# Splitting the first expert matrices beside the second attention, and an unrolled router that sends one row a token

## The chip, the cores and the metric

The kernel runs on one core of one Trainium2 chip. The metric is device time in microseconds (us), the median of several runs; lower is better. A core has five engines that each work through their own instructions in order: TensorE (PE, matmuls and transposes), VectorE (DVE), ScalarE (ACT), GpSimd (POOL) and SyncE (SP, which here only starts DMA transfers). They wait for one another through semaphores, and every wait in this kernel is written by hand.

## The reference

Input `x` is 4 x 1024 tokens of 256 floats. Four blocks follow, each added to `x` after a layer norm: cross attention over 64 context tokens (16 heads), a quantised gated feed-forward, a second cross attention (with low-rank additions, and with the last 4 context tokens as a second softmax group), and a mixture of 8 experts, of which each token uses 2:

```python
    def _L1_ffn_ref(x, Wr, br, W1, b1, W2, b2):
        scores = jnp.einsum('bsd,de->bse', x, Wr) + br
        _, topk_idx = jax.lax.top_k(scores, K)          # K = 2, E = 8
        indicator = jax.nn.one_hot(topk_idx, E, dtype=scores.dtype).sum(-2)
        weights = jax.nn.softmax(jnp.where(indicator > 0, scores, neg_inf), axis=-1)
        for i in range(E):
            xi = x * indicator[..., i:i + 1]
            h = jax.nn.relu(jnp.einsum('bsd,dh->bsh', xi, W1[i]) + b1[i])
            yi = jnp.einsum('bsh,hd->bsd', h, W2[i]) + b2[i]
            out = out + yi * weights[..., i:i + 1]
        return out
```

W1 is 8 x 256 x 1024 and W2 is 8 x 1024 x 256.

## The kernel before, in words

The tokens are cut into 32 tiles of 128. The stages run one after the other: first attention, feed-forward, `prepare_attention` for the second attention, `attention` (second), `route`, `experts`. Between two stages all engines meet.

**Second attention.** Each engine runs a step for each k from -4 on. The body for four tiles (NS = 4, j = k mod 4) is the body of a hardware loop, with the first and the last four tiles written out. In step k, PE computes `scores(k+3)`, turns `x` of tile k+4 (`turn_x`), turns the probabilities of tile k (`turn_probs`), and multiplies them out for tile k-1 (`output`). ScalarE normalises tile k+4, copies the scores of k+3 out of PSUM, takes the upper fp16 halves (`high_x`, `high_p`), does the exponentials of k+2 and then `squares`. VectorE does maxima, sums, inverses, the lower halves (`rest_x`, `rest_p`), the residual and the statistics. GpSimd does `normalise(k+1)`, `subtract(k+3)` and `add_bias(k+4)`, in that order (lines 699 and 712). `squares` (L617) reads half of one expert matrix (128 x 1024 floats) each step, loaded by SP into one of two buffers, and adds up its squares in `ssq`, from which later a power-of-two scale for every matrix is made. The matrices are not kept.

**Route.** `partition_all_reduce` on GpSimd (L1351) finds the maxima over the partitions, VectorE makes the scales, GpSimd then writes constants (from L1352). All 32 halves of the expert matrices are loaded again; ScalarE makes the upper fp16 half (`hi`, L1432), VectorE the lower (`lo`, L1511). Between them the 32 tiles are scored in four chunks of eight (`walk`, a hardware loop): VectorE normalises a tile, PE turns and scores it. After a chunk VectorE takes the two best experts of every token (L1551 to L1563), PE counts (L1417, L1418), and VectorE works out where each row goes in the DRAM buffer `xs`, sorted by expert (up to L1592). During the next chunk, for each tile, `rows` normalises again into `pay` (four buffers, two rows a token: one for each expert, with its weight and the token's number), `copy_rows` doubles it, and GpSimd sends 2 x 128 rows by indirect DMA (L1376).

**Experts.** 39 tiles of 256 rows, each by one expert: PE turns the rows, multiplies by W1 (`up`, L1693) and W2 (`down`, L1706), each as three fp16 products; VectorE weighs the result by the row's weight (`mt`, kept by `keep_meta`), and GpSimd adds the rows to the output by indirect DMA (L1810).

## Time and profile before

| | us |
| --- | --- |
| median of 3 runs (1702.17 to 1707.84) | 1704.43 |
| the profiled execution, its own time | 1706.82 |
| its span, first to last instruction | 1705.0 |
| second attention, first PE instruction to last statistics | 861.8 to 1085.1 |
| routing | 1085.4 to about 1255 |
| first and last matmul of the experts' unbroken chain | 1262.2 to 1685.1 |

Mean granted clock of TensorE over the span is 0.848 of full speed. Busy shares of the span are PE 76%, DVE 64%, ACT 46% and POOL 31%. A share is an average over stages with different limits, so each stage has to be read by itself.

### The profile page before, as it was taken

The page shows a single profiled execution, that of the slowest core. Times are in us where ns is not written, and L with a number is a line of the kernel's source. Part 1 is how long each engine was busy: PE and PEld are TensorE (multiplying, and loading weights), DVE is VectorE, ACT ScalarE, POOL GpSimd, SP SyncE. Part 2 cuts the span into 40 slices and gives each one's busy share as a digit, 9 for nine tenths or more (in the row PEclk, how much of TensorE's full clock was granted, in tenths as well). Part 3 has the DMA queues.
Part 4 walks back from the last instruction along what each step waited for, and adds up shares of the span by engine and source line. Part 5 has one row for each costly group of instructions (what it writes and reads, how often), then busy time and mean ns, then how long its engine had stood idle before and what let it go on. Part 6 is the DMA issues. An engine that isn't in the chain of part 4 may idle for free. (4 is left out here: it accounts for less than half of the span.)

```text
span 1705.0 us, 29650 instructions
## 1 busy us (share of the span) xinstructions
PE 1293.8 (76%) x8779; PEld 956.2 (56%) x8780; DVE 1082.7 (64%) x1994; ACT 782.0 (46%) x1138; POOL 527.4 (31%) x426
## 2 busy tenths in 40 slices
PE   5779999349865008679969999533249999999996
PEld 3337777234322007526527777432239999999895
DVE  6947777685587784335647778567635555555553
ACT  0545665055555677100447777343424343444441
POOL 1046777000000000100037777244522333333333
PEclk9979999669999558855779999755569999999998
DMA  5000000100122440140002222384622322222221
GB/s 189 1 4 1 0 0 0 56 1 0 55 111 111 170 144 1 29 111 0 0 28 87 86 86 77 102 280 148 209 95 45 49 39 46 44 48 46 46 44 12
DMA packets 64938, 110.87 MB, mean 65 GB/s; under 512 B 9904, under 2 KB 50960, under 8 KB 64240
## 3 DMA queue, kind: packets, MB, share of 16 engines
q1 hardware_dynamic: 50576, 93.27, 17.3%
q0 software_dynamic: 14304, 16.87, 5.7%
q8 instruction: 32, 0.52, 0.1%
q14 instruction: 26, 0.21, 0.0%
HBM read 74.10 MB, written 37.83 MB: 66 GB/s over the span
## 5 line engine op out<-in xcount | busy, mean ns | idle before, releaser
L1810 POOL DMA_INDIRECT out<-ex_yo,ex_mt x78 | 137.3, 1760 | 314.4 <-DVE ex_yo L1785 181.4
L1735 ACT ACTIVATE ex_hT<-ex_ps_h,e_b1T,e_unscale 128x256 f32<-128x256 f32 x312 | 150.5, 563 | 115.9 <-PE ex_ps_h L1693 115.9
L549 PE MATMUL at_ps_s<-c_M,at_xnT_hi 128*128 (+1 forms) x512 | 163.1, 402 | 20.6 <-issue 13.5
L571 PE MATMUL at_ps_y<-c_VW,at_pT_hi 128*128 (+1 forms) x1024 | 171.1, 273 | 1.3 <-DVE main_x_res L669 1.3
L1693 PE MATMUL ex_ps_h<-ex_xT_hi,e_w_hi 128*128 128x256 f16 x624 | 171.1, 274 | 0.0
L1693 PE MATMUL ex_ps_h<-ex_xT_lo,e_w_hi 128*128 128x256 f16 x624 | 171.0, 274 | 0.0
L1693 PE MATMUL ex_ps_h<-ex_xT_hi,e_w_lo 128*128 128x256 f16 x624 | 171.0, 274 | 0.0
L1706 PE MATMUL ex_ps_y<-e_w_hi,ex_hT_lo 128*128 x624 | 170.1, 273 | 0.0
L1706 PE MATMUL ex_ps_y<-e_w_lo,ex_hT_hi 128*128 x624 | 170.1, 273 | 0.0
L1706 PE MATMUL ex_ps_y<-e_w_hi,ex_hT_hi 128*128 x624 | 170.1, 273 | 0.0
L641 DVE TENSOR_REDUCE at_mx<-at_sc 128x16 f32<-128x960 f32 (+1 forms) x96 | 80.0, 861 | 116.3 <-ACT at_sc L602 116.3
L699 POOL TENSOR_TENSOR at_sc<-at_sc,at_ri 128x960 f32<-128x960 f32 (+1 forms) x96 | 127.3, 1340 | 59.4 <-DVE at_ri L664 59.4
L699 POOL TENSOR_TENSOR at_sc<-at_sc,at_mx 128x960 f32<-128x960 f32 (+1 forms) x96 | 127.3, 1340 | 57.3 <-DVE at_mx L641 57.3
L571 PE MATMUL at_ps_y<-c_VW,at_pT_lo 128*128 (+1 forms) x512 | 139.6, 273 | 0.0
L1209 PE MATMUL gm_bank<-f_WdT,f_xq 128*128 128x256 f16 x576 | 65.7, 279 | 94.5 <-DVE f_xq L1179 94.5
L602 ACT COPY at_sc<-at_ps_s 128x1024 f32<-128x1024 f32 x64 | 64.8, 1013 | 146.5 <-PE at_ps_s L549 146.5
L1209 PEld LDWEIGHTS gm_bank<-f_WdT,f_xq 128*128 128x128 f16 x576 | 57.7, 100 | 102.8 <-DVE f_xq L1179 95.0
L1769 DVE CAST ex_hT_hi<-ex_hT 128x1024 f16<-128x1024 f32 x78 | 58.2, 746 | 80.5 <-ACT ex_hT L1735 80.5
L571 PEld LDWEIGHTS at_ps_y<-c_VW,at_pT_hi 128*128 128x128 f16 x1024 | 100.0, 98 | 12.7 <-issue 1.8
L549 PE MATMUL at_ps_s<-c_M,at_xnT_lo 128*128 (+1 forms) x256 | 102.4, 400 | 0.0
L933 PE MATMUL gm_bank<-f_xq,f_WuT 128*128 (+1 forms) x288 | 71.0, 406 | 35.2 <-ACT gm_stg L971 35.2
L1771 DVE TENSOR_TENSOR ex_hT_lo<-ex_hT,ex_hT_hi 128x1024 f16<-128x1024 f32 x78 | 95.6, 1225 | 2.7
(273 smaller groups left out, 2914.0 us busy)
## 6 DMA issues: line engine op xcount, KB each, us to landing
at_half<-in_L_ffn_W SPq DMA_DIRECT2D x32, 512.0 KB, 3.6
rt_stage<-in_L_ffn_W SPq DMA_DIRECT2D x32, 512.0 KB
up_scratch<-gm_stg SPq DMA_DIRECT2D x16, 768.0 KB, 3.2
gm_stg<-up_scratch SPq DMA_DIRECT2D x16, 768.0 KB, 4.3
ex_row<-xs SPq DMA_DIRECT2D x39, 258.0 KB, 2.7
main_x_res<-in_x SPq DMA_DIRECT2D x8, 512.0 KB, 12.2
out<-main_x_res SPq DMA_DIRECT2D x4, 1024.0 KB
xs<-rt_pad SPq DMA_DIRECT2D x18, 129.0 KB
```

Source lines behind the costliest of these rows:

```text
L549: last = nc.tensor.matmul(ps_s[j][:, c * CH:(c + 1) * CH], a[:, d, :], b[:, d, bass.ds(off + c * CH, CH)], start=(n == 0), stop=(n == 3 * ...
L571: last = nc.tensor.matmul(ps_y[:, 0:D], a[j][:, n, :], b[:, bass.ds(off + n * D, D)], start=(n == 0 and i == 0), stop=(n == NP - 1 and i = ...
L602: nc.scalar.copy(sc[j][:, :, :], ps_s[j % 2][:, :].rearrange("p (h k) -> p h k", h=H)).then_inc(ev_r, 1)
L641: last = nc.vector.tensor_reduce(mx[:, j, :, g], sc[j][:, :, lo:hi], AX.X, ALU.max)
L699: last = nc.gpsimd.tensor_tensor(part, part, what[:, j, :, g].unsqueeze(2).to_broadcast([P, H, hi - lo]), op)
L933: last = nc.tensor.matmul(ps[:, o, :], a[:, d, o * P:(o + 1) * P], b[:, d, bass.ds(c0, CH)], start=(n == 0), stop=(n == 3 * DT - 1))
L1209: last = nc.tensor.matmul(ps[:, i, 0:D], a[k % 2][:, at], b[:, o, :], start=(o == 0 and n == 0), stop=(o == FT - 1 and n == 2))
L1693: last = nc.tensor.matmul(ps_h[:, n, :], a[:, bass.ds(e * WN + d * HID + n * P, P)], b[:, d, :], start=(m == 0), stop=(m == 3 * DT - 1))
L1706: last = nc.tensor.matmul(ps_y[j][:, q, :], a[:, n, q * P:(q + 1) * P], b[:, bass.ds(e * WN + n * D, D)], start=(n == 0 and m == 0), stop= ...
L1735: last = nc.scalar.activation(hT[:, n, :], ps_h[:, n, :], ACT.Relu, bias=b1T[:, bass.ds(e * HT + n, 1)], scale=unscale[:, 0, bass.ds(e, 1)])
L1771: nc.vector.tensor_tensor(hT_lo[j][:, part, :], hT[:, part, :], hT_hi[j][:, part, :], ALU.subtract).then_inc(hlo_r, 1)
L1810: nc.gpsimd.indirect_dma_start(out=acc[:, :], out_offset=bass.IndirectOffsetOnAxis(ap=mt[j][:, q, 1:2].bitcast(U32), axis=0), in_=yo[j][:, ...
```

## The change

Five edits that belong together.

1. The memory of W1 in fp16 (`w1`) is reserved before the second attention. While `prepare_attention` runs, its weight buffers lie in it (`arena`).
2. In the second attention, expert e's W1 halves and W2 halves are loaded in the four steps of group e (tiles 4e to 4e+3). The W1 halves stay in their buffers. When their squares are known, VectorE adds the two sums (`scale_of`, j = 2), GpSimd takes the maximum over the partitions (j = 3, ahead of `normalise`), VectorE makes the scale from it (`scale_from`, j = 3, ahead of `rest_p`), ScalarE writes the upper halves (`high_w`, j = 3) and VectorE the lower ones (`low_w`, j = 0 of the next group).
3. `route` is written out instead of looped, splits only W2 (16 halves), and ScalarE normalises straight into the buffer that is sent (`pay`, two buffers of eight tiles). Two sends a tile remain, now both from the same row.
4. A row carries 4 extra values: the first expert's number, (first weight - second weight), second weight, token.
5. In `experts`, `keep_meta` works out the weight from the row and the tile's expert.

```diff
@@ attention, SyncE
+                load_half(1, 0, 0)
+                load_half(0, 0, 0)
+                load_half(0, 0, 1)
+                sp.wait_ge(ssq_r, 1)
+                load_half(1, 0, 1)
+                with nc.sync.Fori(1, E, 1) as e:
+                    sp.wait_ge(ssq_r, 4 * e)
+                    load_half(1, e, 0)
+                    for h in range(2):
+                        sp.wait_ge(wlo_r, 2 * e + h - 1)
+                        load_half(0, e, h)
+                    sp.wait_ge(ssq_r, 4 * e + 1)
+                    load_half(1, e, 1)
@@ attention, ScalarE
+            def high_w(e, h):
+                act.wait_ge(scale_r, e + 1)
+                nc.scalar.activation(w1[0][...], half[h][:, :], ACT.Copy, scale=scale1[:, 0:1]).then_inc(whi_r, 1)
+            def weights(e, j):
+                if j == 0:
+                    squares(e, 1, 0)
+                elif j == 1:
+                    squares(e, 0, 0)
+                    squares(e, 0, 1)
+                elif j == 2:
+                    squares(e, 1, 1)
+                else:
+                    high_w(e, 0)
+                    high_w(e, 1)
@@ attention, VectorE
+            def scale_from(e):
+                dve.wait_ge(all_s, e + 1)
...
             def step(k, j):
                 if there(k - 2, NT):
                     residual(k - 2)
+                if experts_w and j == 0 and there(k - NS, NT):
+                    low_w(k // NS, 0)
+                    low_w(k // NS, 1)
+                if experts_w and j == 2 and there(k, NT):
+                    scale_of(k // NS)
...
+                if experts_w and j == 3 and there(k, NT):
+                    scale_from(k // NS)
                 if there(k, NT):
                     rest_p(k, j % 2)
@@ attention, GpSimd
             def step(k, j):
+                if experts_w and j == 3 and there(k, NT):
+                    pool.wait_ge(sum_s, k // NS + 1)
+                    pool.sem_inc(asked, 1)
+                    nc.gpsimd.partition_all_reduce(bmr[:, :], bm[:, :], P, RMAX).then_inc(all_s, 1)
                 if there(k + 1, NT):
                     normalise(k + 1, (j + 1) % NS)
@@ route, GpSimd
+            for t in range(NT):
+                c, i = divmod(t, TK)
+                pool.wait_ge(meta_r, c + 1)
                 for k in range(2):
+                    g.indirect_dma_start(out=xs[:, :], out_offset=bass.IndirectOffsetOnAxis(ap=pos[c % 2][:, i, k:k + 1], axis=0),
+                                         in_=pay[c % 2][:, i, :], in_offset=None, bounds_check=last_row,
+                                         oob_is_err=True).then_inc(sent[c % 2], 16)
@@ route, ScalarE
+            def norm(t):
+                c, i = divmod(t, TK)
+                if i == 0:
+                    need(act, sent[c % 2], 32 * TK * (c // 2))
+                nc.scalar.activation(pay[c % 2][:, i, 0:D], x_res[:, t, :], ACT.Identity, bias=nmr[:, t:t + 1],
+                                     scale=rstd[:, t:t + 1]).then_inc(xn_r, 1)
...
+            norm(0)
+            for t in range(NT):
+                if t + 1 < NT:
+                    norm(t + 1)
+                copy(t)
+                if t == 2:
+                    act.wait_ge(wsc_r, 1)
+                if t % TK in HIGHS:                     # (2, 4, 6, 7)
+                    high(4 * (t // TK) + HIGHS.index(t % TK))
+                if t % TK == 1 and t > TK:
+                    ratio(t // TK - 1)
+            ratio(NK - 1)
@@ route, VectorE
+            for m in range(NK):
+                if m:
+                    place(m - 1)
+                for q in range(4 * m, 4 * m + 4):
+                    low(q)
+                choose(m)
+            place(NK - 1)
@@ experts, VectorE
             def keep_meta(i, j):
+                e = look_up(nc.vector, 1, i, E - 1)
                 need(dve, added, 16 * Q * (i - 1))
                 dve.wait_ge(meta_r, i + 1)
-                nc.vector.tensor_copy(mt[j][:, :, :], meta[j][:, :, :]).then_inc(mt_r, 1)
+                need(dve, mt_r, i)
+                nc.vector.scalar_tensor_tensor(out=first[:, :, :], in0=meta[j][:, :, 0:1], scalar=eid[:, bass.ds(e, 1)],
+                                               in1=meta[j][:, :, 1:2], op0=ALU.is_equal, op1=ALU.mult).then_inc(first_r, 1)
+                nc.vector.tensor_copy(mt[j][:, :, 1:2], meta[j][:, :, 3:4])
+                dve.wait_ge(first_r, i + 1)
+                nc.vector.tensor_tensor(mt[j][:, :, 0:1], first[:, :, :], meta[j][:, :, 2:3], ALU.add).then_inc(mt_r, 1)
```

`choose` is the work of L1551 to L1563 on a whole chunk, `place` that of L1567 to L1592.

## Rows read from the trace of the kernel before

**Rows 1.** The page, busy time of one engine over the span, share, instructions.

```profile
PE 1293.8 (76%) x8779; PEld 956.2 (56%) x8780; DVE 1082.7 (64%) x1994; ACT 782.0 (46%) x1138; POOL 527.4 (31%) x426
```

**Rows 2.** The chain that ended last, in order of time: start, us, what.

```profile
1262.19 1.12 PE ex_ps_t L1679 x4
...
1679.82 5.25 PE ex_ps_y L1706 x48
```

**Rows 3.** Stretches: us, busy PE, PEld, DVE, ACT, POOL (xcount), PEclk, DMA share, GB/s.

```profile
933.00:985.00 52.00, 52.00 (x384) 38.69 (x383) 40.10 (x81) 40.00 (x67) 40.28 (x41) 1.00 0.28 89
1084.00:1256.00 172.00, 48.35 (x210) 43.38 (x209) 107.53 (x467) 60.37 (x103) 74.48 (x75) 0.51 0.58 185
```

**Rows 4.** Timeline of one tile of the second attention: start, us, engine, line.

```profile
951.86 0.38 PE L537 MATMUL at_ps_xT<-main_ident,at_xn 128*128 128x128 f32 x2
952.08 1.04 PE L560 MATMUL at_ps_p<-main_ident,at_sc 128*128 128x128 f32 x8
...
955.57 0.59 PE L549 MATMUL at_ps_s<-c_M,at_xnT_hi 128*128 x2
...
958.16 0.38 PE L537 MATMUL at_ps_xT<-main_ident,at_xn 128*128 128x128 f32 x2
```

**Rows 5.** The same tile on POOL; in brackets the idle time before and its releaser.

```profile
954.54 2.08 POOL L699 TENSOR_TENSOR at_sc<-at_sc,at_mx 128x960 f32<-128x960 f32 x2 [0.53 <-DVE at_mx L641]
956.58 0.73 POOL L712 TENSOR_TENSOR main_x_res<-main_x_res,at_bias 128x256 f32 x1
```

**Rows 6.** Lines 712 and 1351, the queue's own instructions: duration ns, first and last start.

```profile
L712 POOLq MODIFY_POOL_CONFIG  x4: 11/11/11, 85.5 to 861.2; - x4
L1351 POOLq MODIFY_POOL_CONFIG  x2: 11/11/11, 1089.0 to 1089.0; - x2
```

**Rows 7.** Timeline of POOL: what it ran next after those, and after L1351.

```profile
92.77 0.71 POOL L712 TENSOR_TENSOR main_x_res<-main_x_res,at_bias 128x256 f32<-128x256 f32 x1 [45.63 <-issue]
...
870.28 0.71 POOL L712 TENSOR_TENSOR main_x_res<-main_x_res,at_bias 128x256 f32<-128x256 f32 x1 [40.45 <-issue]
...
1095.18 0.43 POOL L1351 PARTITION_ALL_REDUCE rt_bmr<-rt_bm  x1 [18.30 <-issue]
1102.70 0.14 POOL L1352 IOTA rt_eid<- 128x8 f32 x1 [7.08 <-issue]
```

**Rows 8.** Stretches of 2 us after TensorE had stood still (columns as rows 3).

```profile
871.00:873.00 2.00, 1.69 (x5) 0.69 (x6) 0.16 (x1) 0.00 (x0) 2.00 (x3) 0.61 0.00 0
873.00:875.00 2.00, 2.00 (x7) 0.72 (x6) 0.00 (x0) 0.00 (x0) 0.70 (x2) 0.54 0.00 0
...
1266.00:1268.00 2.00, 2.00 (x15) 1.54 (x13) 0.00 (x0) 0.00 (x0) 0.00 (x0) 0.66 0.51 139
```

**Rows 9.** Timeline, the end of the second attention.

```profile
1074.81 2.08 POOL L699 TENSOR_TENSOR at_sc<-at_sc,at_ri 128x960 f32<-128x960 f32 x2 [1.42 <-DVE at_ri L664]
...
1084.66 0.43 DVE L674 BATCH_NORM_STATS2 main_stats<-main_x_res 128x6 f32<-128x256 f32 x1
```

**Rows 10.** Timeline of the routing on DVE and POOL, first chunk, first reuse, last send.

```profile
1092.55 0.22 DVE L1472 COPY e_b1T<-rt_ps_r 128x64 f32<-128x64 f32 x1 [4.08 <-PE rt_ps_r L1389]
...
1114.36 0.64 DVE L1551 MAX8 rt_top<-rt_scores 128x8 f32<-128x8 f32 x8
...
1122.87 0.18 DVE L1592 CAST rt_pos<-rt_posf 128x16 uint32<-128x16 f32 x1
...
1125.65 1.33 POOL L1376 DMA_INDIRECT xs<-rt_pay,rt_row  x1 [21.36 <-issue]
...
1133.83 0.41 DVE L1460 TENSOR_SCALAR rt_pay<-main_x_res,main_mv,main_rstd 128x256 f32 x1 [0.83 <-DMA xs<-rt_pay,rt_row]
...
1246.90 0.97 POOL L1376 DMA_INDIRECT xs<-rt_pay,rt_row  x1 [0.30 <-issue]
```

**Rows 11.** Groups by line: count, busy us, mean ns, idle before and releasers.

```profile
L1376 POOL DMA_INDIRECT xs<-rt_pay,rt_row x64 | 72.5, 1133 | 71.0 <-issue 38.1 <-ACT rt_pay L1437 22.5 <-DVE rt_row L1521 10.5
L1511 DVE SCALAR_TENSOR_TENSOR e_w_lo<-rt_stage,rt_wsc,e_w_hi 128x1024 f32 (+1 forms) x32 | 41.1, 1284 | 7.1 <-ACT e_w_hi L1432 6.1 <-issue 0.7
```

More of the change, by code:

```diff
@@ L497, in attention @@
         if experts_w:
-            half = [s.sb(f"half{j}", [P, WN // 2]) for j in range(2)]
-            half_in = [s.sem(f"half_in{j}") for j in range(2)]
-            ssq_r, arrived = s.sem("ssq_r"), s.sem("arrived")
+            half = [s.sb(f"half{j}", [P, WN // 2]) for j in range(3)]
+            half_in = [s.sem(f"half_in{j}") for j in range(3)]
+            bm, bmr, scale1 = s.sb("bm", [P, 1]), s.sb("bmr", [P, 1]), s.sb("scale1", [P, 1])
+            asked = s.sem("asked")
+            ssq_r, arrived, sum_s, all_s, chain, scale_r, whi_r, wlo_r = (
+                s.sem(n) for n in ("ssq_r", "arrived", "sum_s", "all_s", "chain", "scale_r", "whi_r", "wlo_r"))
         block = s.block()
@@ L1235, in route @@
         b1r = s.sb("b1r", [E * HT, P])
-        xn = s.sb("xn", [P, 2, D])
+        pay = [s.sb(f"pay{j}", [P, TK, ROW]) for j in range(2)]
         xt = [s.sb(f"xt{j}", [P, DT, P]) for j in range(2)]
@@ L1258, in route @@
         hp, hs = s.sb("hp", [P, E]), s.sb("hs", [P, E])
-        pay = [s.sb(f"pay{j}", [P, 2, ROW]) for j in range(NB)]
-        row_i = [s.sb(f"row{j}", [P, 2], U32) for j in range(NB)]
         pad = s.sb("pad", [P, ROW])
@@ L1326, in _ @@
-            with nc.sync.Fori(1, 2, 1) as e:
-                for j in range(2):
-                    load_matrix(e, j)
+                need(sp, wlo_r, q - NS + 1)
+                sp.dma_start(stage[q % NS][:, :].rearrange("p (t n) -> p t n", n=src.shape[2]),
+                             src[q // 2, (q % 2) * rows:(q % 2 + 1) * rows, :].rearrange("(t p) n -> p t n", p=P)
+                             ).then_inc(half_in[q % NS], 16)
+            for q in range(NS):
+                load_half(q)
@@ L1332, in _ @@
                              x_res[:, g * NT // B:(g + 1) * NT // B, :]).then_inc(acc_in, 16)
-            with nc.sync.Fori(2, E, 1) as e:
-                for j in range(2):
-                    load_matrix(e, j)
+            for q in range(NS, 2 * E):
+                load_half(q)
             sp.wait_ge(cst, CONSTS)
@@ L1402, in score @@
                 for d in range(DT):
-                    last = nc.tensor.matmul(ps_r[j][:, 0:E], xt[j][:, d, :], wr[:, d, :], start=(d == 0), stop=(d == DT - 1))
+                    last = nc.tensor.matmul(ps_r[c % 2][:, i * E:(i + 1) * E], xt[t % 2][:, d, :], wr[:, d, :],
+                                            start=(d == 0), stop=(d == DT - 1))
                 last.then_inc(sc_mm, 1)
-            def tile_step(i, r, t, half):
-                if t is not None:
-                    turn(t, i % 2)
-                    if i >= 1:
-                        score(t - 1, 1 - i % 2)
@@ L1454, in _ @@
+            for t in range(NT):
+                if t + 1 < NT:
[8 more added lines that the diff above has]
+            ratio(NK - 1)
         @block.vector
@@ L1523, in tile_step, with low @@
-            def tile_step(i, r, t, half):
-                if r is not None:
-                    rows(r, i)
-                if t is not None:
-                    norm(t, i % 2)
-                    if i >= 2:
-                        score(t - 2, i - 2)
-                if half:
-                    lo(*half)
-            LINKS = 15
-            def chunk_step(c):
-                for i in range(TK - 2, TK):
-                    score(TK * c + i, i)
-                dve.wait_ge(sc_r, TK * (c + 1))
-                k = [0]
-                def then(ins):
-                    k[0] += 1
-                    ins.then_inc(link, 1)
-                    dve.wait_ge(link, LINKS * c + k[0])
-                    dve.sem_inc(linked, 1)
-                dve.sem_inc(linked, 1)
+            def low(q):
+                dve.wait_ge(whi_r, q + 1)
+                v.scalar_tensor_tensor(out=half_of(1, q), in0=stage[q % NS][:, :], scalar=wsc[:, 1, q // 2:q // 2 + 1],
+                                       in1=half_of(0, q), op0=ALU.mult, op1=ALU.subtract).then_inc(wlo_r, 1)
@@ L1551, in chunk_step @@
                     last = v.max(out=top[:, i, :], in_=scores[:, i, :])
-                then(last)
+                link_on(last)
                 v.tensor_tensor(wt[:, 0, :], top[:, :, 1], top[:, :, 0], ALU.subtract).then_inc(d_r, 1)
@@ L1622, in experts @@
         row = [s.sb(f"row{j}", [P, Q, ROW]) for j in range(2)]
-        meta = [s.sb(f"meta{j}", [P, Q, 2]) for j in range(2)]
+        meta = [s.sb(f"meta{j}", [P, Q, 4]) for j in range(2)]
+        first = s.sb("first", [P, Q, 1])
         mt = [s.sb(f"mt{j}", [P, Q, 2]) for j in range(2)]
```

309 lines of the change are left out of this document (144 added, 165 removed).

## The prediction

> **What bounds the kernel now.** I read the page first, then the chain that ended last, then stretches of single stages, then timelines inside them. The page gives PE 76% of the span [rows 1], which is an average. The chain says more: from 1262.2 to 1685.1 it is nothing but PE, matmul after matmul [rows 2]. Nothing that the change adds to VectorE's 39 steps there can cost time as long as it stays within VectorE's slack. So the change has to be judged in the two stages ahead of the experts, which are bound differently [rows 3]. In the second attention PE is busy 52.0 of 52 us at full clock, with VectorE at 40.1, ScalarE at 40.0 and GpSimd at 40.3. In the routing PE has 48 of 172 us at a clock of 0.51 (its lower level, 1.2 GHz), and no engine is full: VectorE has 107.5, ScalarE 60.4 and GpSimd 74.5. Work moved from the routing into the attention goes from a stage where engines wait for each other into one that has 12 us in 52 left on each engine but PE.
>
> A tile of that attention lasts 6.30 us (951.86 to 958.16): `turn_x` 0.22, `turn_probs` and `output` 3.49, `scores` 2.59 [rows 4]. GpSimd's share is 2 x 2.08 + 0.73 = 4.89 us, and the last of it ends 957.31 - 951.86 = 5.45 us after the scores that it needed, through ScalarE's copy and VectorE's maxima [rows 4, 5].
>
> **The change part by part.**
>
> *The reduction on GpSimd inside the attention.* This decides. The line that reduces over partitions is preceded in GpSimd's queue by MODIFY_POOL_CONFIG, and so is the first elementwise instruction of each attention, which follows such a reduction [rows 6]. The instruction itself takes 11 ns, but what comes next is late: 85.5 to 92.77 is 7.3 us, 861.2 to 870.28 is 9.1, 1089.0 to 1095.18 is 6.2, and after the reduction at 1095.61 the first constant starts at 1102.70, 7.1 later [rows 6, 7]. I read this as GpSimd changing its resident code, 6.2 us towards the reduction and 7.1 to 9.1 back (mean 7.8). Before, nobody waits long for it, since it happens between stages. After the change the reduction stands between elementwise work in every group of four tiles, so both switches come in each: 6.2 + 0.43 + 7.8 = 14.4 us in which GpSimd does nothing else (13.7 to 15.7). It is followed in the queue by `normalise`, `subtract` and `add_bias`; for `normalise` waits `turn_probs`, and with it PE.
>
> The Trainium skill ("GPSIMD Engine Reference", 2.1 Instruction dispatch) says that the first call into freshly loaded code costs about 6 us (5.95) with no instruction to be seen. The trace agrees for the way there and shows 1.1 to 3.1 us more for the way back. By the page a group would lose 2.1 us less, and the sum below would be 15 lower.
>
> How much of 14.4 us reaches PE? Let the stall begin after step K-1. PE has then still two tiles' work, 12.6 us, counted from the end of the scores that GpSimd's last step used, and those ended 5.45 us before. So it runs 7.2 us into the stall and stops at `turn_probs(K+1)`. Count from the stall's end. `normalise` takes 2.1. PE then needs `turn_probs` and `output` (3.49), `scores` (2.59), 0.22, again 3.49 and 2.59 until the last scores of the group: 12.4. It starts after 9 us of standing still, so at the lower clock. Two restarts of before show for how long: from 871.31 to about 874.8 (0.54 over the stretch that ends at 875) and from 1262.19 to about 1267.4, thus 3.5 to 5.2 us, in which half the speed is lost: 1.7 to 2.6, I take 2.2 [rows 2, 8]. Then 5.45 until GpSimd's last instruction, and the next stall begins: 2.1 + 12.4 + 2.2 + 5.45 = 22.15. GpSimd's own work, 4 x 4.89 = 19.6, is less, so PE's restart sets it. With the stall a group takes 36.5 us, against 4 x 6.30 = 25.2: +11.35. Groups 0 to 6 have elementwise work after the reduction: 7 x 11.35 = +79.5.
>
> In group 7 only the way there counts, but `scale_from` stands ahead of the last `rest_p` in VectorE's queue and `low_w` ahead of the last residual. Before, the last `normalise` ended at 1076.89 and the last statistics at 1085.09 [rows 9]. After: 1076.9 + 6.2 + 0.43, some 0.9 for four small operations, 1.3 `rest_p`, PE's 2.6 at the lower clock 5.2, 0.9 for residual and statistics: 1091.8, so +6 (by the full clock +4).
>
> *The splits in the attention.* Per group ScalarE and VectorE each get two passes over 128x1024, 2 x 1.28 by VectorE's row, and VectorE about 0.9 more for the scale [rows 11], on top of 19.4 each in 25.2 [rows 3]. Both fit, and they lie in the stall: `scale_from` waits for the reduction, 6.6 us into it, `high_w` and `low_w` end before it is over. Cost 0; if the stall were not there, they would still fit, at most 2 us a group if `low_w` delays an inverse that GpSimd waits for. The number of squares is as before. The loads are as many bytes as before, each asked for about a tile ahead of its use: 0.
>
> *Routing.* Before, the 64 sends take 72.5 us plus 0.3 each, 91.7, and GpSimd idles 31.4 between chunks (22.5 + 10.5 less the 0.3s) [rows 11]. They begin at 1125.65 [rows 10]. After, chunk 0 no longer passes through VectorE. b1 is turned by 1092.6 as before, then PE and ScalarE need about 1.7 us a tile (an estimate: ScalarE has two passes over 128x256, 0.41 each on VectorE, and half of one of 1.28, and hands over to PE twice), so the last scores stand near 1107 instead of 1114. The fourth `low` ends by 1108.8. `choose` and `place` took from just before 1114.36 to 1123.05, about 9: 1117.9. Nothing like `rows` follows, so sends begin near 1118, 7.7 earlier. But `pay` holds two chunks, and `norm(16)` stands on ScalarE ahead of `copy(15)`: the second chunk can't be scored until all sends of the first have landed, and the third's transfers hold up chunk 3's end in the same way. Landing: the first buffer was free at 1133.83, 8.2 us after its two sends began, of which 2.6 to 3.6 were the sends; I take 4.8. From there: normalise and copy 1.0, `high(7)` and `low(7)` 1.28 each, `choose` and `place` 9: 12.6. So GpSimd stands 17.4 us twice, 34.8 against 31.4, and not a third time (chunk 3 is placed while chunk 2 is sent). Net -7.7 + 3.4 = -4.3. Bounds: if every send takes 0.97 + 0.3 as the last does [rows 10], -10 more, so -15; if a tile takes 2.1 us and a gap 20, +4. The first reduction finds its code resident, which only brings the scales 2 us forward, ahead of need.
>
> *Experts.* Three small VectorE operations of about 0.17 for one, +0.35 us on a tile whose PE work takes 10.9 [rows 2]: 0. If VectorE were the bound it would be 39 x 0.35 = 14. The rows are 0.8% longer: 0.
>
> Sum: +79.5 + 6 - 4.3 = +81.2. On the profiled execution's own 1706.82 that is 1788.0; the median of the runs is 2.4 lower, which gives 1785.6; I forecast 1785.
>
> **The rivals.**
>
> *A: the switches cost nothing in the loop.* Both pieces of code stay resident, or the reduction is reached without the pair of switches. For it: the trace has no reduction between elementwise instructions, so none was seen in a loop. Against: all four such neighbours in the trace are 6.2 us or more apart [rows 6, 7]. Then PE stays the attention's bound, +2 at its end, and the routing's -4 to -15 shows: 1704.4 + 2 - 4 = 1702 down to 1704.4 - 15 = 1689, in the middle 1696. This is the other side. It decides from the point where a stall falls below about 7 us, since PE has 7.2 us of work in hand.
>
> *B: only one of the two directions costs.* Stall 7.8: PE waits 2.7, keeps its clock, and a group takes 2.1 + 12.4 + 5.45 + 7.8 = 27.7: +2.5, 7 times 17.5. 1704.4 + 17.5 + 4 - 4 = 1722. For it: the shorter numbers could be a queue draining; against, the way there and the way back are both seen.
>
> *C: the clock does not come back inside a group.* Standing still 9 us in 36, PE might get 0.5 all through: 12.4 more on its path instead of 2.2, so +10.2 x 7 = 71: 1785 + 71 = 1856. Against: both restarts came back to 1.0 within 5.2 us [rows 8]. The Trainium skill ("TensorE: Matmul & The Clock Gate", HAM oscillation) has kernels that start every pass cold because each is followed by a wait; by that rule this case would lie between my forecast and C.
>
> *D: GpSimd's own work is the bound.* PE restarts at full clock and VectorE or ScalarE are never late: period 19.6 + 13.7 = 33.3, +8.1 x 7 = 57, +4 - 4: 1761.
>
> **How the numbers follow.** Forecast 0.76, A 0.05, B 0.05, C 0.06, D 0.08. The forecast's own range: stall 13.7 to 15.7 is -5 to +9, clock loss 1.7 to 2.6 is -4 to +3, routing -10 to +9, so 1766 to 1806. With D, part of C and steps that I have left out: 1752 to 1826 for 8 in 10. A change within 0.3% (5 us) could not be told from none in a kernel whose three runs spread by 5.7. Faster is A, 0.05; same, 0.01; slower 0.94.
>
> **What would show it.** Right: in the attention's timeline GpSimd has two gaps of 6 to 9 us around each of eight reductions (one at the eighth), PE stands about 9 us in a group, the clock dips once a group, and the stage is longer by 80 to 90 us. In the routing the sends come in three blocks (16, 16, 32) with two gaps near 17 us. The experts' chain is unbroken and as long as before. Wrong: no gap beside the reductions (A); one only (B); PE at 0.5 through the stage (C); a send block before 1110 in the old stage's time, or three gaps, or `ex_ps_h` waiting for VectorE.

## The result, and the profile after

The changed kernel takes 1774.14 us (median of 3 runs, 1772.86 to 1775.33) against 1704.43: a ratio of 1.041, 95% interval [1.038, 1.044], so 69.7 us slower. The forecast was 1785 with 1752 to 1826 as its range. In some executions, of the kernel before too, the second attention begins 12 or 13 us later, which has nothing to do with the change, so what follows is read mainly by the lengths of stages.

| stage (profiled execution of each) | before | after | predicted |
| --- | --- | --- | --- |
| second attention, first PE instruction to last statistics | 223.3 | 313.4 (+90.2) | +85.5 |
| last statistics to first matmul of the experts' chain | 177.1 | 154.2 (-22.9) | -4.3 |
| experts' unbroken chain | 422.9 | 423.1 | 0 |

The total is 11 us below the forecast. It came that close partly by luck: the attention was underestimated by 4.7 us and the routing's gain by 18.6, and the two errors have opposite signs.

Below is the page of the changed kernel, busy time of one engine over the span (beside [rows 1]): the sums have hardly moved, and nothing in them tells of 70 us.

```profile
PE 1317.9 (74%) x8779; PEld 969.1 (55%) x8780; DVE 1072.1 (60%) x1961; ACT 787.2 (44%) x1138; POOL 519.8 (29%) x434
```

The stretch of 147 us in the middle of the second attention shows it (columns as in [rows 3], where 52 us had PE at 52.0): PE is busy for 76% of it, and its mean granted clock is 0.86.

```profile
943.00:1090.00 147.00, 111.16 (x725) 79.34 (x724) 91.12 (x185) 85.88 (x136) 77.01 (x82) 0.86 0.18 56
```

The cause stands in GpSimd's queue. First the queue's own instructions (duration, first and last start), to be held against [rows 6]. MODIFY_POOL_CONFIG comes in pairs: 16 times ahead of the eight reductions, and 14 times ahead of the elementwise product that follows seven of them (behind the eighth no elementwise work is left in the stage).

```profile
L793 POOLq MODIFY_POOL_CONFIG  x16: 8/14/22, 905.8 to 1160.3; - x16
L793 POOL PARTITION_ALL_REDUCE at_bmr<-at_bm x8: 377/377/378, 911.6 to 1165.9; - x8
L774 POOLq MODIFY_POOL_CONFIG  x14: 82/83/83, 911.9 to 1135.3; - x14
```

Then GpSimd's timeline around one of them (beside [rows 5, 7]). `add_bias` ends at 979.39. Six microseconds later the reduction runs for 0.38 us, and 6.71 us after that the next product. Between 979.4 and 992.5 GpSimd does 0.38 us of work.

```profile
978.66 0.73 POOL L787 TENSOR_TENSOR main_x_res<-main_x_res,at_bias 128x256 f32 x1
985.40 0.38 POOL L793 PARTITION_ALL_REDUCE at_bmr<-at_bm  x1 [6.01 <-issue]
992.49 2.07 POOL L774 TENSOR_TENSOR at_sc<-at_sc,at_ri 128x960 f32<-128x960 f32 x2 [6.71 <-DVE at_ri L707]
```

The bracket names VectorE, and that needs a look, because VectorE's own work stands behind the reduction too: the scale, `rest_p`, the residual, `low_w`, the sums, and only then the inverse `at_ri` that the product needs.

```profile
992.12 0.33 DVE L707 RECIPROCAL at_ri<-at_sm 128x32 f32<-128x32 f32 x1
```

Here the inverse ends at 992.45 and GpSimd starts 0.04 us later, so in this one group VectorE may set the end of the wait. In all seven groups the inverse comes 6.5 to 6.7 us after the reduction, and in the other six GpSimd starts 0.24 to 0.83 us after it. The first experiment settles what GpSimd alone needs.

And TensorE through the same stall, against [rows 4]. It stands still twice: 3.72 us until ScalarE's norm, 4.86 until GpSimd's product. The eight transposes that took 1.04 us take 1.94, since the clock is at its lower level (the stretches below), and the next tile's transposes start 9.08 us later in place of 6.30.

```profile
989.52 0.44 PE L555 MATMUL at_ps_xT<-main_ident,at_xn 128*128 128x128 f32 x2 [3.72 <-ACT at_xn L609]
994.81 1.94 PE L578 MATMUL at_ps_p<-main_ident,at_sc 128*128 128x128 f32 x8 [4.86 <-POOL at_sc L774]
...
1003.89 1.04 PE L578 MATMUL at_ps_p<-main_ident,at_sc 128*128 128x128 f32 x8
```

Stretches of 2 us (beside [rows 8]) show when the clock falls and when it is back: 1.00 until 990, 0.50 from 992 to 1000, 1.00 from 1002.

```profile
988.00:990.00 2.00, 0.44 (x2) 0.20 (x2) 2.00 (x3) 2.00 (x3) 0.00 (x0) 1.00 0.00 0
990.00:992.00 2.00, 0.00 (x0) 0.00 (x0) 2.00 (x4) 0.64 (x2) 0.00 (x0) 0.55 0.66 176
...
998.00:1000.00 2.00, 2.00 (x12) 1.41 (x10) 0.11 (x1) 1.95 (x4) 2.00 (x3) 0.50 0.00 0
1000.00:1002.00 2.00, 2.00 (x14) 1.34 (x13) 0.60 (x2) 0.00 (x0) 2.00 (x3) 0.89 0.63 167
```

The end of the attention (against [rows 9]): VectorE waits 5.89 us for the last reduction, works off the scale, and stands 2.74 again for PE's last output. From the end of the last normalisation to the end of the last statistics it is 15.0 us; before it was 8.2.

```profile
1166.30 0.15 DVE L727 TENSOR_SCALAR at_scale<-at_bmr 128x1 f32<-128x1 f32 x1 [5.89 <-POOL at_bmr L793]
...
1174.08 0.48 DVE L712 SCALAR_TENSOR_TENSOR main_x_res<-at_ps_y,c_unscale,main_x_res 128x256 f32<-128x256 f32 x1 [2.74 <-PE at_ps_y L589]
1174.60 0.43 DVE L717 BATCH_NORM_STATS2 main_stats<-main_x_res 128x6 f32<-128x256 f32 x1
```

The routing on GpSimd, against [rows 10]: the first send of each of the three blocks (16, 16 and 32 sends), then the instruction on ScalarE that opens the third chunk, 1.5 us after the first block's last send ended at 1225.03.

```profile
1203.69 2.07 POOL L1408 DMA_INDIRECT xs<-rt_pay,rt_pos  x1 [7.62 <-DVE rt_pos L1594]
...
1237.54 1.76 POOL L1408 DMA_INDIRECT xs<-rt_pay,rt_pos  x1 [12.51 <-DVE rt_pos L1594]
...
1271.18 1.75 POOL L1408 DMA_INDIRECT xs<-rt_pay,rt_pos  x1 [12.72 <-DVE rt_pos L1594]
```

```profile
1226.52 0.60 ACT L1460 ACTIVATE rt_pay<-main_x_res,main_nmr,main_rstd 128x256 f32<-128x256 f32 x1 [18.98 <-DMA xs<-rt_pay,rt_pos]
```

The group of the sends, answering to the first of [rows 11]: 65.2 us in place of 72.5, and 51.5 us of idle time before them in place of 71.0 (7.6 of the 51.5 lie ahead of the first send).

```profile
L1408 POOL DMA_INDIRECT xs<-rt_pay,rt_pos x64 | 65.2, 1019 | 51.5 <-DVE rt_pos L1594 32.9 <-issue 18.6
```

The experts' chain, as in [rows 2], is unbroken and as long as before.

```profile
1329.25 1.11 PE ex_ps_t L1685 x4
...
1747.13 5.25 PE ex_ps_y L1712 x48
```

### The profile page after: what moved, and what is told of

Its sections match the earlier page's. It is cut to its first block and busy times, and to the rows that moved or that the text cites. A ratio compares the mean times of both kernels' runs of the same rounds, so it can differ in the third digit from the quotient of the medians.

```text
span 1772.4 us, 29247 instructions
## 1 busy us (share of the span) xinstructions
PE 1317.9 (74%) x8779; PEld 969.1 (55%) x8780; DVE 1072.1 (60%) x1961; ACT 787.2 (44%) x1138; POOL 519.8 (29%) x434
## 5 line engine op out<-in xcount | busy, mean ns | idle before, releaser
L589 PE MATMUL at_ps_y<-c_VW,at_pT_hi 128*128 (+1 forms) x1024 | 186.0, 287 | 5.6 <-DVE main_x_res L712 5.6
L567 PE MATMUL at_ps_s<-c_M,at_xnT_hi 128*128 (+1 forms) x512 | 161.6, 399 | 20.7 <-issue 13.5
L589 PE MATMUL at_ps_y<-c_VW,at_pT_lo 128*128 (+1 forms) x512 | 146.3, 286 | 0.0
L589 PEld LDWEIGHTS at_ps_y<-c_VW,at_pT_hi 128*128 128x128 f16 x1024 | 105.5, 103 | 21.9 <-issue 6.1
L578 PE MATMUL at_ps_p<-main_ident,at_sc 128*128 128x128 f32 x512 | 72.9, 290 | 43.2 <-POOL at_sc L774 43.2
L1732 ACT ACTIVATE ex_xT_hi<-ex_ps_t 128x512 f16<-128x512 f32 x39 | 23.3, 597 | 182.4 <-PE ex_ps_t L1685 182.4
L1773 DVE SCALAR_TENSOR_TENSOR ex_xT_lo<-ex_ps_t,ex_xT_hi 128x512 f16<-128x512 f32 x39 | 26.9, 690 | 124.0 <-ACT ex_xT_hi L1732 124.0
```

The source lines that it names most:

```text
L567: last = nc.tensor.matmul(ps_s[j][:, c * CH:(c + 1) * CH], a[:, d, :], b[:, d, bass.ds(off + c * CH, CH)], start=(n == 0), stop=(n == 3 * ...
L578: last = nc.tensor.transpose(ps_p[:, n, :], sc[j][:, 2 * n:2 * n + 2, :], ident[:, :])
L589: last = nc.tensor.matmul(ps_y[:, 0:D], a[j][:, n, :], b[:, bass.ds(off + n * D, D)], start=(n == 0 and i == 0), stop=(n == NP - 1 and i = ...
L1773: nc.vector.scalar_tensor_tensor(out=xT_lo[j][:, :, :], in0=ps_t[:, :, :], scalar=XN_SCALE, in1=xT_hi[j][:, :, :], op0=ALU.mult, op1=ALU.s ...
```

## The experiments

Ratios are to the kernel before, run beside each on the same chip. The lengths compared are the attention from PE's first instruction in it to the last statistics (223.3 before, 313.4 after), a group of four tiles from reduction to reduction (four tiles of 6.30, 25.2, before; 37.2 after, (1134.94 - 911.55)/6), and the routing.

Two theories on the attention's 90 us. The first is the prediction's: GpSimd changes its code twice a group. The rival: the splits of W1 crowd ScalarE and VectorE, and the tiles wait for them.

**The reductions alone, in the kernel before.**

```
+                if experts_w and j == 3 and there(k, NT):
+                    nc.gpsimd.partition_all_reduce(red[:, :], one[:, :], P, RMAX).then_inc(red_r, 1)
                 if there(k + 1, NT):
                     normalise(k + 1, (j + 1) % NS)
```

> The kernel before, plus one partition_all_reduce of a one-column tile on GpSimd in the second attention, ahead of the normalisation of every fourth tile (eight in all); nothing waits for its result, and nothing else is changed. Theory 1 (changes of code alone): groups of four tiles of 36 to 37.5 us, total 1704 + 7 x 12 + 7 = 1785 to 1797. Theory 2 (splits and their waits crowd the engines): at most 0.4 us a reduction, total 1704 to 1712.

Measured: 1786.14 us, ratio 1.046 [1.040, 1.053]. The attention takes 299.4 us (+76.1), a group 36.3 on average, (1142.26 - 924.40)/6, single ones 35.4 to 37.0. The stall is there with nothing that waits for a result, as the timeline of GpSimd in this kernel shows (in brackets the idle time before each): 6.50 and 7.04 us around 0.38.

```profile
1069.66 0.38 POOL L717 PARTITION_ALL_REDUCE at_red<-at_one  x1 [6.50 <-ACT at_xn L592]
1077.08 2.07 POOL L700 TENSOR_TENSOR at_sc<-at_sc,at_ri 128x960 f32<-128x960 f32 x2 [7.04 <-issue]
```

Here nothing of VectorE's holds the product back (its inverse is ready within 0.5 us of each reduction), and the way back still takes 7.04 to 7.50 us in all seven groups. So VectorE's queue is not what makes the 7 us. And 76 of the 90 us come with eight reductions of one column that nobody reads. The rival can have 14 at most.

**A second reduction behind the first.**

```
                     nc.gpsimd.partition_all_reduce(bmr[:, :], bm[:, :], P, RMAX).then_inc(all_s, 1)
+                    nc.gpsimd.partition_all_reduce(red[:, :], bm[:, :], P, RMAX).then_inc(red_r, 1)
```

> The changed kernel with a second partition_all_reduce right behind the first in each group, into a tile that nobody reads. If the price is in going from one code to the other and back, the second reduction costs its own 0.4 us: total 1774 + 8 x 0.4 = 1775 to 1780. If each reduction has the price by itself, it is paid twice: 1774 + 7 x 12 = 1850 or more; if only its first half (6 us) belongs to the reduction, about 1815.

Measured (one run): 1778.20 us; attention 313.8, +0.4 on the changed kernel. GpSimd's timeline shows the two reductions back to back and the same 7 us behind them:

```profile
986.19 0.38 POOL L794 PARTITION_ALL_REDUCE at_bmr<-at_bm  x1 [6.04 <-issue]
986.48 0.42 POOL L795 PARTITION_ALL_REDUCE at_red<-at_bm  x1
993.96 2.07 POOL L775 TENSOR_TENSOR at_sc<-at_sc,at_ri 128x960 f32<-128x960 f32 x2 [7.06 <-DVE at_ri L708]
```

The price lies in passing from one kind of instruction to the other and back, not in the reduction: paid twice, it would have given 1850 us.

**The sum over partitions on TensorE.** The splits stay where they are.

```
+            def over_partitions(e):
+                pe.wait_ge(sum_s, e + 1)
+                nc.tensor.matmul(ps_xT[:, D:D + 1], ones[:, :], bm[:, :], start=True, stop=True).then_inc(all_s, 1)
...
-                    nc.gpsimd.partition_all_reduce(bmr[:, :], bm[:, :], P, RMAX).then_inc(all_s, 1)
```

> The changed kernel with the reduction of each expert's squares taken off GpSimd: TensorE multiplies a matrix of ones by the partitions' sums (one matmul of one column, beside the turning of x), VectorE reads the result from PSUM; the splits stay where they are. The bound becomes the sum over partitions in place of the largest, and route takes W1's powers of two from where the attention stored them. Theory 1 (GpSimd's two changes of code a group, about 6.0 + 0.4 + 7.1 = 13.5 us, made nearly all of the 90 us that the second attention grew): no MODIFY_POOL_CONFIG between tiles, groups of four tiles back to about 25 us, attention within 8 us of before, routing as in the changed kernel (23 shorter than before), total 1680 to 1692. Theory 2 (the splits crowd ScalarE and VectorE, and this would show without the switches too): groups of 30 us or more, total 1720 to 1765.

Measured: 1697.03 us, ratio 0.995 [0.992, 0.998]. The attention is 231.9 us: 81.5 of the 90.2 are gone. It is 8.6 over before where I had said within 8, and the total missed my 1680 to 1692 by 5 us, since the splits are not free once the stall no longer covers them. A group takes 26.4: two tiles of 6.30, one of 6.48, in which the sum's matmul stands, and one of 7.34. In that one PE stands 0.86 us ahead of its scores, behind VectorE, which has the two `low_w` (2.67 us) on top of its usual 5 us in that step. PE's timeline in this kernel:

```profile
939.85 1.04 PE L585 MATMUL at_ps_p<-main_ident,at_sc 128*128 128x128 f32 x8
...
944.37 0.60 PE L574 MATMUL at_ps_s<-c_M,at_xnT_hi 128*128 x2 [0.86 <-issue]
...
947.19 1.04 PE L585 MATMUL at_ps_p<-main_ident,at_sc 128*128 128x128 f32 x8
```

**No split of W1 at all.**

```
-                    high_w(e, 0)
-                    high_w(e, 1)
...
-                    low_w(k // NS, 0)
-                    low_w(k // NS, 1)
```

> The changed kernel without the split of W1 in the second attention: no scale, no reduction, no high and no low halves; the squares stay, and the experts compute with what lies in w1 (so the output is not the reference's). Theory 1: attention at or below before's length (groups of 25.2 us or a little less), total 1677 to 1686; what it is faster than the kernel whose sum is made by TensorE is the price of the splits beside attention, and I expect 0 to 6 us. Theory 2: 40 us or more faster than that kernel.

This kernel leaves out the scale, its sum and both halves of the split, so its output is not the reference's. Measured: 1685.98 us, ratio 0.987 [0.981, 0.993]; attention 221.4, groups of 25.2. The splits with their sum on TensorE therefore cost 10.5 us beside attention (231.9 - 221.4): 1.2 in each whole group and 3 in the last. That is more than the 0 to 6 expected, and far from the rival's 40.

**TensorE kept busy through the stall.** This was to isolate the clock.

```
+            def keep_busy(t, j):
+                pe.wait_ge(ev_r, t + 3)
+                w = M[0][:, 0, 0, 0:D]
+                for i in range(75):
+                    last = nc.tensor.matmul(ps_s[j % 2][:, 0:D], w[:, 0:P], w, start=True, stop=True)
```

> The changed kernel, with 75 matmuls of 256 columns (about 8 us at the clock of 2.4 GHz) on TensorE ahead of the turning of the probabilities of every fourth tile, in the stretch in which it sits idle behind GpSimd's stall; they write a PSUM buffer that the next scores overwrite. If the clock's fall behind the stall costs what I took (about 2.2 to 2.9 us of slow work a group): granted clock 1.0 throughout the attention, groups of 34 to 35 us in place of 37.2, total 1774 - 7 x 2.9 = 1754 (1750 to 1760). Rival: the slow work lies under other waits, total 1770 to 1776; or the fillers themselves hold TensorE's queue beyond the stall: slower.

Measured: 1783.06 us, ratio 1.050 [1.045, 1.054]; attention 324.3, 10.9 longer than after. This is the last of the cases that I had named, fillers that hold TensorE's queue: I had put them behind the wrong wait. PE's timeline in this kernel: after the scores it sat idle 3.66 us for ScalarE's norm, which is queued behind `high_w` and so behind the scale, and only then did the 75 matmuls start. They ended on the path at 1004. The tile behind the stall did take 6.30 us again, but a group took 38.4 to 39.9.

```profile
994.20 0.69 PE L556 MATMUL at_ps_xT<-main_ident,at_xn 128*128 128x128 f32 x2 [3.66 <-ACT at_xn L619]
994.68 9.60 PE L586 MATMUL at_ps_s<-c_M 128*128 128x256 f16 x75
1004.12 1.04 PE L579 MATMUL at_ps_p<-main_ident,at_sc 128*128 128x128 f32 x8
```

With 26 of them ahead of that wait and 32 behind it:

```
+                if stalled:
+                    keep_busy(k, j, 26)
                 if there(k + 4, NT):
                     turn_x(k + 4, j % 2)
+                if stalled:
+                    keep_busy(k, j, 32)
```

> The changed kernel with the filler matmuls on TensorE in two parts: 26 (3.3 us at the 0.128 us that one took in the run with 75) ahead of the turning of x of every fourth tile, where TensorE sits idle for 3.7 us until ScalarE's norm, which is queued behind the high halves and their scale, and 32 (4.1 us) between it and the turning of the probabilities, where it sits idle for 4.9 us until GpSimd's product. Both fit into idle time this time; in the run with 75 in one piece they began only behind the first wait and ended 9.4 us after TensorE would have gone on. If the slow stretch behind the stall costs 2 to 3 us a group: clock 1.0 throughout, groups of 34.3 to 35.3 us, total 1754 to 1761. If it lies under other waits: 1772 to 1778.

Measured: 1764.72 us, ratio 1.032 [1.026, 1.038]; attention 300.0, 13.4 less than after; a group 35.2 in place of 37.2. The groups came as expected on average; the total is 4 over the upper end, and the clock did not stay up throughout. In four of the six groups it did, and the tile behind the stall took 6.33 us; in two it still fell, and that tile took 8.00. Below are the six whole groups, from reduction to reduction, in this kernel (first) and in the changed one: the mean clock goes from 0.86 to 0.98.

```profile
911.79:1122.83 211.04, 195.44 (x1456) 146.64 (x1455) 138.06 (x282) 129.79 (x204) 117.16 (x127) 0.98 0.20 60
```

```profile
911.55:1134.94 223.39, 169.96 (x1108) 121.07 (x1105) 138.42 (x282) 129.75 (x204) 117.38 (x127) 0.86 0.19 57
```

So useless matmuls in idle time bring 2.1 us a group. That is most of what hangs on the clock: in the changed kernel the tile behind the stall takes 8.92 us on average (8.19 to 9.28), 2.6 more than 6.30.

**The order of the routing.** The changed routing has two gaps. Is it the drain of the sends, or the work that is queued behind the wait for the buffer?

```
+                held = (t + 1) % TK == 0 and t > TK
-                if t + 1 < NT:
+                if t + 1 < NT and not held:
                     norm(t + 1)
                 copy(t)
...
+                if held:
+                    ratio(t // TK)
+                    if t + 1 < NT:
+                        norm(t + 1)
```

(and likewise on TensorE: the last scores and the ranks of a block ahead of the next block's first turning.)

> The changed kernel with only the order in route changed: where the next block's first row would be written into a buffer whose rows are still being sent, ScalarE, TensorE and VectorE first finish the block before it (last copy, scores, ranks, exp), so that its sends are ready when the sends of the other buffer end. Theory (the two gaps of 12.6 us are choose and place held behind the wait for the buffer): first gap gone, second at most 7 us, routing 13 to 20 us shorter, total 1754 to 1761; attention as in the changed kernel. Rival (the gap is the drain of the sends or the work of choosing itself): 1770 or more.

Measured: 1748.10 us, ratio 1.028 [1.024, 1.032]. The sends, first to last, take 86.0 us in place of 109.1. With the new order the second chunk's first send follows at once, after 0.30 us in place of 12.51, the third's after 0.54 in place of 12.72, and the fourth's, which had followed at once, after 1.80. In this kernel they are:

```profile
1235.15 0.98 POOL L1408 DMA_INDIRECT xs<-rt_pay,rt_pos  x1 [0.30 <-issue]
...
1256.95 0.97 POOL L1408 DMA_INDIRECT xs<-rt_pay,rt_pos  x1 [0.54 <-DVE rt_pos L1602]
...
1279.03 0.97 POOL L1408 DMA_INDIRECT xs<-rt_pay,rt_pos  x1 [1.80 <-DVE rt_pos L1602]
```

The gap was the queueing. The whole routing is 25 us shorter than in the changed kernel, above the 20 that I had allowed: the third chunk, too, was ready in time.

**VectorE beside the sends.** Why did the sends get shorter (mean 1133 to 1019 ns, both with a median of 974)? Work on VectorE was added beside the last of them, once with a wait after every operation (the edit below), once in unbroken rows of four, which also read and write other buffers.

```
+            for i in range(6):
+                then(v.scalar_tensor_tensor(out=stage[0][:, :], in0=stage[1][:, :], scalar=wsc[:, 1, 0:1],
+                                            in1=half_of(0, 0), op0=ALU.mult, op1=ALU.subtract))
+            for i in range(20):
+                then(v.tensor_scalar(stage[0][:, 0:D], x_res[:, 0, :], nmr[:, 0:1], rstd[:, 0:1], ALU.subtract, ALU.mult))
```

> The changed kernel with work on VectorE added behind the end of its own routing work, beside the last 25 or so sends, nobody waiting: 6 operations of 128x1024 (the form of the low halves), then 20 of 128x256 (the form of the layer norm of the kernel before). In the kernel before 19 of 64 sends took over 1.1 us (up to 1.92), in the changed one 4 (the first of each of the three blocks, 2.07, 1.76 and 1.75, and one of 1.12), the rest about 0.97. Theory (a send that meets such work on VectorE is stretched): the sends beside the added work are 1.1 to 2.1 us, total 3 to 8 us longer than 1774. Rival (the lengths come from the form of the rows or the loop): all of them stay at 0.97, total 1774 within noise.

> As the kernel with work on VectorE beside the last sends, but the work comes in unbroken rows of four operations with no wait between them: 2 x 4 of 128x1024 and 5 x 4 of 128x256, beside sends from about 1287 us on. With a wait after each operation one send took 1.94 and eleven 1.01 to 1.11. Theory (a send that meets an unbroken row of VectorE's operations is held until the row has a gap): 3 to 8 sends of 1.3 us or more, as in the kernel before (16 of 64). Rival: 1.0 to 1.1 as before with at most one long.

Measured: 1784.31 and 1783.93 us, one run each. In both the attention already begins late (at 874.7 and 873.6 in place of 861.6), so the totals don't tell; the lengths of the sends do. (In the kernel before 14 sends took 1.3 us or more, not 16.) With a wait after each operation one send took 1.94 us, then five 1.01 to 1.02 and six 1.10 to 1.11. With unbroken rows six sends ran beside the eight wide operations (9.81 us): three took 1.94, 2.02 and 2.02, the other three 0.97 to 1.01. Those beside the narrow ones took at most 1.12. GpSimd's timeline in the latter kernel, and VectorE's beside it:

```profile
1296.97 1.94 POOL L1408 DMA_INDIRECT xs<-rt_pay,rt_pos  x1 [0.30 <-issue]
1299.21 0.97 POOL L1408 DMA_INDIRECT xs<-rt_pay,rt_pos  x1 [0.30 <-issue]
1300.49 2.02 POOL L1408 DMA_INDIRECT xs<-rt_pay,rt_pos  x1 [0.30 <-issue]
```

```profile
1296.78 9.81 DVE L1623 SCALAR_TENSOR_TENSOR rt_stage<-main_x_res,rt_wsc,e_w_hi 128x1024 f32<-128x1024 f32 x8
1306.63 7.42 DVE L1628 TENSOR_SCALAR rt_stage<-main_x_res,main_nmr,main_rstd 128x256 f32<-128x256 f32 x20
```

So unbroken wide operations on VectorE hold some sends for about 1 us: half of them here, against one of six with the waits. What decides which send is held is open: the one of 0.97 us began beside the third wide operation, with no gap ahead of it or behind. The middle lengths of before (1.2 to 1.55 us) did not come back, so their cause is open too, and with it a part of the 7.3 us by which the sends got shorter.

**Both mended.** The sum on TensorE, the new order in the routing, and one of the two `low_w` of a step moved to its end.

```
                 if experts_w and j == 0 and there(k - NS, NT):
                     low_w(k // NS, 0)
-                    low_w(k // NS, 1)
...
+                if experts_w and j == 0 and there(k - NS, NT):
+                    low_w(k // NS, 1)
                 if there(k, NT):
                     rest_p(k, j % 2)
```

> Sum on TensorE in place of GpSimd's reduction, the new order in route, and VectorE's second low half moved from the start of its step to ahead of the step's last operation (in the kernel with the sum on TensorE one tile in four took 7.3 us in place of 6.3, TensorE waiting 0.86 us ahead of its scores). 1697 less 13 to 20 for the order in route less 7 x 1.0 for the moved half: 1672 to 1680. If the half only moves the wait: 1678 to 1684.

Measured: 1662.19 us, ratio 0.978 [0.974, 0.982]: 2.2% faster than before, with 1.8 to 2.6% as the interval, and 10 us under the forecast of 1672 to 1680. The attention is 225.6 us (6.4 less than with both halves at the start), the sends 86.1, the whole routing 129.3. TensorE's wait ahead of the experts ends at 1217.60; in the changed kernel it was 1329.25:

```profile
1217.60 1.11 PE L1713 MATMUL ex_ps_t<-main_ident,ex_row 128*128 128x128 f32 x4 [2.31 <-DMA ex_row<-xs]
```

## Why the prediction held, point by point

**The code switch of GpSimd: right.** I took 6.2 + 0.43 + 7.8 = 14.4 us. The changed kernel has a mean of 6.05 + 0.38 + 7.11 = 13.5 over seven groups, below the 13.7 that I gave as the lower end. The way back was taken from two starts behind a whole stage (7.3 and 9.1) and one in the routing (7.1) [rows 6, 7]; in the loop it is near the smallest of them. That the stall comes with passing to the reduction and back is shown by the reductions alone (+76.1) and by the second reduction (+0.4). That what passes is resident code is my reading of MODIFY_POOL_CONFIG; no run looks inside.

The Trainium skill ("GPSIMD Engine Reference", 2.1 Instruction dispatch) gives 5.95 us for the first call into freshly loaded code. The way to the reduction agrees (5.95 to 6.18); the way back is again about 1.1 longer. The page speaks of a first call. This kernel pays at every alternation in the loop: eight times on the way there and seven on the way back.

**A group: 36.5 predicted, 37.2 measured, by errors that cancel.** The part behind the stall was to be 2.1 + 12.4 + 2.2 + 5.45 = 22.15. It is 37.2 - 13.5 = 23.7 after, and 36.3 - 14.05 = 22.3 in the kernel with the reductions alone, whose stall is a mean of 6.46 + 0.38 + 7.21. So the stall was 0.9 too long in my sum and the rest 1.5 too short. Two of its terms were mis-sized.

The first is the 5.45, which I took over from before. VectorE now begins the third step of a group with `scale_of`, and that waits for ScalarE's squares, 1.2 to 1.35 us a group. Everything behind it in VectorE's queue is late, the inverse too, and GpSimd's last instruction ahead of the stall ends 0.92 us later against PE than before. I had given the scale a price (0.9 us of work) and no wait. First VectorE's and GpSimd's timeline in the changed kernel, then GpSimd's in the kernel with the reductions alone:

```profile
1009.52 0.16 DVE L721 TENSOR_TENSOR at_bm<-main_ssq 128x1 f32 x1 [1.33 <-ACT e_w_hi L640]
1011.53 2.08 POOL L774 TENSOR_TENSOR at_sc<-at_sc,at_ri 128x960 f32<-128x960 f32 x2 [2.42 <-DVE at_ri L707]
```

```profile
1021.11 2.08 POOL L700 TENSOR_TENSOR at_sc<-at_sc,at_ri 128x960 f32<-128x960 f32 x2 [0.92 <-DVE at_ri L665]
```

The second is the clock, 2.2 us in my sum. The tile behind the stall takes 8.92 us on average after, 2.6 over 6.30, and 8.41 with the reductions alone, 2.1 over. So of the 1.4 us between the two kernels 0.9 is the wait for the squares and 0.5 the clock. How long the low level lasts differs from group to group, though PE stands equally long: with the reductions alone it stands 8.7 to 9.1 us in one piece, and after the restart the clock is low for 2.8 us in two groups and for 4.2 to 5.8 in the others. After, with the wait in two pieces, it is 3.8 to 6.1. One of the long cases with the reductions alone:

```profile
1079.40 1.94 PE L561 MATMUL at_ps_p<-main_ident,at_sc 128*128 128x128 f32 x8 [8.71 <-POOL at_sc L700]
```

```profile
1083.00:1085.00 2.00, 2.00 (x12) 1.39 (x10) 0.00 (x0) 1.54 (x4) 2.00 (x3) 0.50 0.00 0
1085.00:1087.00 2.00, 2.00 (x13) 1.20 (x12) 0.95 (x2) 0.00 (x0) 1.62 (x3) 0.96 0.84 193
```

And a short one, in which PE went on at 1007.26:

```profile
1008.00:1010.00 2.00, 2.00 (x11) 1.68 (x10) 0.83 (x2) 1.37 (x3) 2.00 (x4) 0.50 0.00 0
1010.00:1012.00 2.00, 2.00 (x20) 1.75 (x18) 0.55 (x1) 2.00 (x4) 2.00 (x3) 0.98 0.00 0
```

Why it differs is not settled. The step "it starts after 9 us of standing still" also overlooked that ScalarE's norm is queued behind `high_w`, which cut the wait in two. It cost nothing that the runs show, but it undid the first of the two runs with TensorE kept busy.

**The end of the attention: right.** +6.8 against +6.

**The splits: cost 0 under the stall, and a cover that was worth more than I said.** Without the stall they cost 10.5 us, within the "at most 2 us a group" that I gave for that case. Under the stall they still showed: 90.2 - 76.1 = 14.1, of which 6.8 is the end and about 7 the groups, mostly the wait for the squares. "Cost 0" was a near thing, too: `high_w` and `low_w` do end before the stall is over, but the inverse queued behind `low_w` comes 6.7 us after the reduction, 0.04 to 0.83 us before GpSimd starts. With that order in VectorE's queue a shorter way back could have gained 0.83 us a group at most.

**The routing: the mis-sized term.** -22.9 against -4.3, outside my bounds of -15 to +4. The mechanism was right (three blocks of 16, 16 and 32, two gaps, the second chunk held by `norm(16)` ahead of `copy(15)`); the sizes were not:

- the first send comes 28.7 us after the last statistics in place of 40.6: 11.9 earlier, not 7.7. `choose` began 20.7 us after the last statistics, not 23.7, and with `place` took 7.6 us (1195.77 to 1203.36), not 9.
- a gap is 12.6 us, not 17.4. I took 4.8 us for the landing of a send from a row that only bounds it from above: VectorE was busy until 1133.0 and stood 0.83 us [rows 10], and 0.95 and 0.78 ahead of the next two. Landing took 1.5 us here (1225.03 to 1226.52), and from there to the next send it was 11.0 in place of 12.6.
- the sends take 65.2 us in place of 72.5. I had that in the bound (-10 for a send of 0.97 each) and not in the sum. VectorE is mostly idle beside the sends now, and the runs with work added beside them show it holding some of them; the rest of the difference is open.
- behind the last send 2.2 us more.

Together -11.9 - 6.2 (two gaps of 12.6 for 31.4) - 7.3 + 2.2 = -23.2, for -22.9 measured.

The Trainium skill ("SBUF — State Buffer", Who interferes with whom) says that VectorE and GpSimd share a pair of ports as an exclusive lock, and that a VectorE instruction with two inputs in SBUF contends with GpSimd's reads. The trace agrees in part: beside the unbroken wide rows, with two inputs in SBUF, three of six sends were held for about 1 us, and the other three were not. The narrow operations, with one tensor input, cost a send 0.14 us.

**The experts: right**, +0.2 us for three more small operations a step.

**The rivals.** A is excluded: the stall in a loop is 13.5 us, well over the 7 that PE has in hand. B is excluded: the way there is seen eight times and the way back seven. C did not come: the clock is back at 1.0 within each group, and its mean over the groups is 0.86. D would have needed a restart that costs nothing. Even with TensorE kept busy a group is 35.2, above D's 33.3. The Trainium skill ("TensorE: Matmul & The Clock Gate", HAM oscillation) has kernels that start every pass cold because each is followed by a wait; the trace agrees, with the clock down in each of the seven groups, and each cold start costs 1.4 to 3.0 us here and not C's 12.4.

## What to carry to other kernels

A cross-partition reduction on GpSimd between elementwise work costs two changes of code, 13.5 us here for 0.38 us of work, in every turn of the loop. A second reduction right behind the first cost 0.4 us, so reductions belong together; or take the sum by a matmul with ones, which cost about 0.2 us a group (one tile of 6.48 in place of 6.30). A neighbour's stall hides work that is not free: measure the price of the moved work with the stall gone before calling it nothing. An operation of 0.16 us at the head of a step can cost more by its wait than by its work: `scale_of` made every group 0.9 us longer. And where a buffer's reuse is waited for in program order, look at what of the current block is queued behind that wait: finishing it first was worth 25 us at no cost.

## What the runs showed of the hardware

The way back from the reduction is longer than the way there. In the changed kernel the way there is 5.95 to 6.18 us in the seven groups and the way back 6.91 to 7.49 in the six in which VectorE's inverse was clearly ready first; with the reductions alone, where nothing else is waited for, it is 6.30 to 6.54 there and 7.04 to 7.50 back. Behind the routing's reduction the way back to the first constant is 9.3 us in the changed kernel (1184.50 to 1193.82) and was 7.1 before, so it is not one number; why is open. A second reduction behind the first pays nothing but its 0.42 us. A filler matmul of 256 columns took 0.115 us at the higher clock (3.00/26 in the run with two parts); the 75 in one piece took 0.128 each (9.60/75), since the clock was at 0.50 for their first 2.5 us. After idle stretches of the same 8.7 to 9.1 us the granted clock came back 2.8 us after the restart in two groups and up to 5.8 us after it in others.
